# A shared expert in high and low products, and a router spread over other chunks of the step

## The chip, the cores and the metric

The kernel runs on one core of a Trainium2 chip. The metric is the device time of one execution in microseconds (us). The engines named are TensorE (PE, its weight loads PEld), VectorE (DVE), ScalarE (ACT), GpSimd (POOL) and SyncE (SP), whose queue issues most DMA transfers.

## What is computed

The input x is 128 sequences of 128 rows of 256 numbers, and so is the context. The layer is a cross attention with a difference of two softmaxes, and then a mixture of experts with two chosen of 16 and one shared expert. Cut to what matters:

```python
x = x + xattn(ctx, layernorm(x))          # 32 half heads of 8, 16 heads
x = x + moe(layernorm(x))

def moe(x):
    shared = silu(x @ ws_gate) * (x @ ws_up) @ ws_down
    scores = sigmoid(x @ gate_w.T)
    topk_w, topk_idx = top_k(scores, 2)
    topk_w = topk_w / (topk_w.sum(-1) + 1e-20) * 2.5
    routed = sum over the two chosen experts of topk_w * expert(x)
    return routed + shared
```

The change concerns `shared`, `scores` and the choice of the two experts.

## The kernel before

The work has two parts. The first and longer one is a software pipeline over 64 pairs of sequences (256 rows each). A step of it runs the attention of one pair `it` and, beside it, earlier and later stages of other pairs: the projections of pair it + 3 (called a), the values and the maxima of pair it + 1 (b), the second normalization of pair it - 1 (d), and the router and shared expert of pair it - 2 (r). The second part runs the routed experts over 288 tiles of rows; the change does not touch it.

Each step has 16 chunks, k = 0 to 15. In every chunk TensorE first does four products for the maxima of pair b (L493, bank `mx_ps`) and four for the scores of pair it (L486, bank `st_ps`), which stand alternately. VectorE reduces the first to maxima (L981), ScalarE takes the exponential of the second (L825). In odd chunks TensorE then multiplies with the values (L526, eight records in the trace). After that comes the side work of the chunk, written in `side(it, k)` for TensorE, and in a `step` function of its own for each other engine. Each engine runs its list strictly in order; counting semaphores tie the lists together. The banks for scores and maxima are double, so TensorE in chunk k needs the maxima of chunk k - 2 reduced.

Two more banks of PSUM, `ms_ps` 0 and 1 (M0 and M1 in the code), are shared by all side work in turn. `clear(it, bank, n)` makes TensorE wait for whoever read the bank last. M0 holds in turn the values of pair b, the logits, the result of the shared down layer, the ranks, and the keys of pair a. M1 holds the transposed rows of pair a, the shared gate and up results, the queries of pair a, and the transposed normalized rows of pair d.

The side work that matters here, before the change:

- chunk 2: a transpose of maxima (L542), which ScalarE copies (L797) and SyncE sends by DMA (L369) into the stacks of the scores; TensorE waits for it to land ahead of chunk 8.
- chunk 3: the gate layer of the shared expert (L575, two full float32 products over the two halves of the input rows; they show as four records), then the logits (L582).
- chunk 4, 7, 12, 15: four transposes of attention outputs (L537).
- chunk 5: the up layer (L575). ScalarE takes tanh of the gate (L854), VectorE makes the hidden layer in its chunk 6 with two instructions (L1025 to `sh_g`, L1028 to `sh_h`), which read M1, and the best two experts in chunk 7 (L1040 to L1048), the choice in chunk 8 (L1053), the addition of the down result to the residual in chunk 9 (L1035).
- chunks 8 and 9: the down layer, one full product each (L605), into M0.
- chunks 9 and 10: the query projection of pair a into M1, each a set of six products of high and low parts (L554, L555, L556, twice). Such a set is already used for all three attention projections and for the routed experts.
- chunk 11: the ranks (L601, L602). Chunks 13 and 14: the key projection into M0.

`product` multiplies high by high, high by low and low by high parts of rounded operands. The high parts are copies by ScalarE into the rounded type, the low parts differences by VectorE or GpSimd. The bank rule of M1 reads:

```python
"M1": (((v_x, 1, a, 1),), ((v_sh, 1, r, 1),), ((v_q, 1, a, 1),), ((a_h, 1, d, 1),)),
```

Its second entry is the wait ahead of the query projection: for the hidden layer of pair r.

Of the kernel before, what the change touches and what calls it, by code (L numbers as in the profile page):

```python
# [13 lines left out]
ALU = mybir.AluOpType  # L14
# [51 lines left out]
def program(nc, x, ctxT, lq1, lk1, lq2, lk2, wqT, wkT, wvT, gate_wT, w_gu, w_dn, ws_gu, ws_dn, out):  # L66
# [31 lines left out]
    with ExitStack() as st:  # L98
# [19 lines left out]
        ws_dn_sb = sb("ws_dn_sb", [P, D])  # L118
        in_lo = e_lo[:, :, :, :].rearrange("p e k n -> p (e k n)")
# [127 lines left out]
        v_rt, v_hot, v_pf, v_pos, v_next = sem("v_rt"), sem("v_hot"), sem("v_pf"), sem("v_pos"), sem("v_next")  # L247
# [5 lines left out]
        v_base, g_ve1, g_ve2 = sem("v_base"), sem("g_ve1"), sem("g_ve2")  # L253
# [3 lines left out]
        N_SPLIT = 3  # L257
# [74 lines left out]
        split_w = [(w_in[:, n, :, :], w_hi[:, n, :, :], w_lo[:, n, :, :]) for n in range(3)]  # L332

# [141 lines left out]
        def _(pe):  # L475
            pe.wait_ge(d_w, 16 * N_W)
            pe.wait_ge(g_set, SETUP)
            pe.wait_ge(v_wl, N_SPLIT)
# [107 lines left out]
            def clear(it, bank, n):  # L586

                a, b, d, r = it.plus(3), it.plus(1), it.plus(-1), it.plus(-2)
                users = {"M0": (((a_v, 1, b, 1),), ((a_e, 1, r, 1),), ((v_base, 1, r, 1),), ((v_pf, 1, r, 1),),
                                ((a_k, 2, a, 2),)),  # L590
                         "M1": (((v_x, 1, a, 1),), ((v_sh, 1, r, 1),), ((v_q, 1, a, 1),), ((a_h, 1, d, 1),)),
# [12 lines left out]
            def shared_down(bank, u):  # L604
                return pe.matmul(bank[:, u * D:(u + 1) * D], sh_h[:, u * P:(u + 1) * P], ws_dn_sb[:, :], start=True, stop=True)  # L605

            def finish():
# [6 lines left out]
                pe.wait_ge(v_sh, NS - 1)  # L614
# [15 lines left out]
                pe.wait_ge(v_sh, NS)  # L630
# [5 lines left out]
            def side(it, k):  # L636
# [15 lines left out]
                alone = it.k is None and it.off >= NS  # L652
                if k == 3 and do_r:
                    wait(pe, a_h, 1, r, 1)
                    if alone:
                        clear(it, "M0", 1)
                        route()
                if k in (3, 5) and do_r:
                    if k == 3:
                        clear(it, "M1", 1)  # L660
                    mm = gate_up(k // 2 - 1)
                    if k == 5:
                        mm.then_inc(p_su, 1)
# [804 lines left out]
```

## Time and profile before

| | us |
|---|---|
| median of 3 runs | 2138.11 |
| lowest and highest | 2124.88, 2149.83 |
| profiled execution | 2130.88 |
| its span, first to last instruction | 2129.1 |
| TensorE busy | 1967.5 (92%) |
| VectorE, ScalarE, GpSimd busy | 1616.4, 1464.5, 1441.6 |

The trace gives each instruction's start and length on its engine, and for idle time ahead of an instruction what ended it. Matmuls overlap in the engine, so what one costs is read from the start of one to the start of the next, and not from its length.

### The profile page before, as it was taken

The numbers are of one execution on the slowest core, as the hardware profiler recorded it, in microseconds if no ns is written. First come the engines' busy times: TensorE is split into PE (matmuls) and PEld (weight loads), VectorE is DVE, ScalarE is ACT, GpSimd is POOL, SyncE is SP. The second block draws the span as 40 slices with busy tenths as digits, with TensorE's granted clock in tenths as the row PEclk, the third lists the DMA queues.
The fourth block names the chain that finished last, engine by engine and source line by source line (L and its number), as shares of the span: only waits on it lengthen the run. The fifth ranks groups of instructions, "written<-read, shape, count | busy, mean of one in ns | idle before, by whom it ended". The sixth has DMA issues, their size and how long they took to land.

```text
span 2129.1 us, 76257 instructions
## 1 busy us (share of the span) xinstructions
PE 1967.5 (92%) x20840; PEld 1418.7 (67%) x20840; DVE 1616.4 (76%) x4623; ACT 1464.5 (69%) x3511; POOL 1441.6 (68%) x2183
## 2 busy tenths in 40 slices
PE   3899999999999999999999999999989699999997
PEld 2555666666666666666666666666655599989996
DVE  2667788888778878888788887778776777767775
ACT  2567778777778777787787877777766455545554
POOL 4346677777677777677777777777656566656665
PEclk8799999999999999999999999999999799999999
DMA  4766676667666767666667676666774688868885
GB/s 122 195 189 194 186 199 189 203 203 199 190 185 196 204 189 196 194 195 194 198 194 201 190 200 193 192 190 191 212 211 161 206 266 263 259 200 274 256 267 172
DMA packets 606681, 432.00 MB, mean 203 GB/s; under 512 B 437572, under 2 KB 552395, under 8 KB 606161
## 3 DMA queue, kind: packets, MB, share of 16 engines
q1 hardware_dynamic: 546288, 319.87, 54.4%
q0 software_dynamic: 32256, 84.47, 10.9%
q10 hardware_dynamic: 28000, 26.03, 4.0%
q8 instruction: 64, 1.05, 0.2%
q14 instruction: 73, 0.59, 0.1%
HBM read 234.59 MB, written 197.72 MB: 203 GB/s over the span
## 4 chain that ended last, share of the span: by engine, by line
PE 54%; DMA 15%; SPq 14%; issue 7%; DVE 6%; POOL 3%; ACT 1%; DVEq 0%; POOLq 0%; ACTq 0%
DMA stacks<-mxT 8%; PE mx_ps L493 8%; SPq L369 7%; PE o_ps L526 6%; PE ms_ps L777 5%; PE ms_ps L554 5%; SPq L361 3%; SPq L354 3%; DMA stack_dram<-w_dn_sb 3%; PE mx_ps L554 3%; DMA stacks<-stack_dram 3%; PE mx_ps L556 3%; PE mx_ps L555 3%; PE ms_ps L555 3%; PE st_ps L755 3%
## 5 line engine op out<-in xcount | busy, mean ns | idle before, releaser
L981 DVE TENSOR_REDUCE mx<-mx_ps 128x4 f32<-128x512 f32 x1024 | 696.6, 686 | 234.4 <-PE mx_ps L493 229.7
L825 ACT ACTIVATE prob<-st_ps 128x512 f32<-128x512 f32 x1024 | 607.7, 596 | 318.4 <-PE st_ps L486 299.0
L493 PE MATMUL mx_ps<-stacks 48*128 48x128 bf16 x4096 | 397.7, 221 | 84.3 <-DMA stacks<-mxT 62.9
L486 PE MATMUL st_ps<-stacks 50*128 50x128 bf16 x4096 | 397.0, 221 | 0.0
L493 PEld LDWEIGHTS mx_ps<-stacks 48*128 48x128 bf16 x4096 | 232.4, 95 | 240.6 <-issue 130.5
L526 PE MATMUL o_ps<-prob,v_sb 128*32 128x256 f32 x4096 | 334.0, 398 | 0.9 <-ACT oT L812 0.6
L1343 POOL DMA_INDIRECT rows_dram<-rowt,posi x256 | 253.7, 991 | 67.9 <-issue 63.7
L554 PE MATMUL ms_ps<-e_lo 128*128 128x256 f32 x768 | 269.5, 351 | 18.6 <-DVE rowt L1080 9.8
L486 PEld LDWEIGHTS st_ps<-stacks 50*128 50x128 bf16 x4096 | 230.6, 95 | 2.6 <-issue 1.5
L555 PE MATMUL ms_ps<-e_lo 128*128 128x256 f32 x768 | 222.8, 290 | 0.0
L556 PE MATMUL ms_ps<-e_lo 128*128 128x256 f32 x768 | 221.8, 289 | 0.0
L554 PEld LDWEIGHTS ms_ps<-e_lo 128*128 128x128 f32 x768 | 151.0, 197 | 100.3 <-issue 44.6
L922 ACT ACTIVATE rows_T<-st_ps 128x256 fp32r<-128x256 f32 x288 | 110.7, 385 | 140.0 <-PE st_ps L755 136.8
L1412 POOL DMA_INDIRECT sums_dram<-stacks x144 | 141.7, 984 | 81.2 <-issue 65.4
L1416 POOL DMA_INDIRECT out<-stacks x144 | 141.7, 984 | 79.3 <-issue 64.3
L554 PE MATMUL mx_ps<-e_hi,rows_T 128*128 x576 | 188.2, 327 | 0.0
L1206 DVE TENSOR_TENSOR rows_lo<-st_ps,rows_T 128x256 fp32r<-128x256 f32 x288 | 122.3, 425 | 80.9 <-ACT rows_T L922 59.1
L1349 POOL DMA_INDIRECT base_dram<-base_t,posi x128 | 139.1, 1087 | 53.0 <-issue 51.0
L777 PE MATMUL ms_ps<-w_dn_sb,v_sb 128*128 x576 | 172.8, 382 | 0.4 <-DVE stacks L1219 0.3
L537 PE MATMUL o_ps<-ident,oT 128*128 128x128 f32 x1024 | 168.1, 287 | 0.6 <-issue 0.4
L556 PE MATMUL mx_ps<-e_hi,rows_lo 128*128 x576 | 163.7, 284 | 0.0
L555 PE MATMUL mx_ps<-e_lo,rows_T 128*128 x576 | 163.4, 284 | 0.0
(155 smaller groups left out, 4667.3 us busy)
## 6 DMA issues: line engine op xcount, KB each, us to landing
stacks<-stack_dram SPq DMA_DIRECT2D x512, 192.0 KB
stack_dram<-w_dn_sb SPq DMA_DIRECT2D x192, 256.0 KB
stacks<-rows_dram SPq DMA_DIRECT2D x288, 130.0 KB
stack_dram<-w_dn_sb SPq DMA_DIRECT2D x64, 384.0 KB
stack_dram<-w_dn_sb SPq DMA_DIRECT2D x192, 128.0 KB
w_dn_sb<-in_x SPq DMA_DIRECT2D x64, 256.0 KB
w_dn_sb<-in_ctxT SPq DMA_DIRECT2D x64, 256.0 KB, 3.2
x_res<-in_x SPq DMA_DIRECT2D x64, 256.0 KB
```

Source lines behind the costliest of these rows:

```text
L369: sp.dma_start(q_st[s.par()][row:row + 2, u, :, :], mxT[u][2 * SHH * h:2 * SHH * (h + 1), :]).then_inc(d_m[u], 16)
L486: return pe.matmul(st_ps[k % 2][:, i * P:(i + 1) * P], k_st[p][64 * h:64 * h + KROWS, u, j, :], q_st[p][64 * h:64 * h + KROWS, u, j, :], s ...
L493: return pe.matmul(mx_ps[k % 2][:, i * P:(i + 1) * P], q_st[p][64 * h:64 * h + ROWS, u, j, :], k_st[p][64 * h:64 * h + ROWS, u, j, :], sta ...
L526: mm = pe.matmul(OT[SLOT * g:SLOT * (g + 1), gg * SW:(gg + 1) * SW], v_sb[s.par()][:, (u * HEADS + 2 * c + i) * SLOT:(u * HEADS + 2 * c + ...
L537: mm = pe.transpose(out_ps, src, ident[:, :])
L554: pe.matmul(out_ps, rnd(still[0]), rnd(moving[0]), start=start, stop=False)
L555: pe.matmul(out_ps, rnd(still[0]), rnd(moving[1]), start=False, stop=False)
L556: return pe.matmul(out_ps, rnd(still[1]), rnd(moving[0]), start=False, stop=stop)
L777: pe.matmul(eo_ps[t.off % 2][:, 0:D], hid_T[t.off % 4][:, :], w_dn_sb[:, bass.ds(down, 1), :].rearrange("p e n -> p (e n)"), start=True, s ...
L825: nc.scalar.activation(prob[k % 4][:, :], st_ps[k % 2][:, :], ACT.Exp, scale=float(HALF) ** -0.5).then_inc(a_exp, 1)
L981: v.tensor_reduce(mx[:, u, c * CHUNK:(c + 1) * CHUNK], mx_ps[k % 2][:, :].rearrange("p (c n) -> p c n", c=CHUNK), AX.X, ALU.max).then_inc( ...
L1343: g.indirect_dma_start(rows_dram[k][:, :], bass.IndirectOffsetOnAxis(ap=posi[p][:, u, k:k + 1], axis=0), rowt[p][:, u, :], None).then_inc( ...
```

## The change

The three layers of the shared expert become sets of products of high and low parts. New tiles are `gu_hi`, `gu_lo`, `dn_hi`, `dn_lo` for the weights (split once, early), `h2_hi`, `h2_lo` for the normalized rows, and `sh_hi`, `sh_lo` for the hidden layer. ScalarE makes the high part of the rows in its chunk 2, ahead of the copy of maxima, and that of the hidden layer in its chunk 9. GpSimd makes the low part of the rows (`normed_low`) after its third residual piece, VectorE the low part of the hidden layer in its chunk 10.

On TensorE the logits go from chunk 3 to chunk 4, gate and up from 3 and 5 to 5 and 6, the ranks from 11 to 9, and the down layer, both halves together, from 8 and 9 to 12. On VectorE the best two go to chunk 6, the choice to 7, the hidden layer to 8, the places from 12 to 10, the positions from 13 to 11, the addition from 9 to 12. Semaphores that were no longer needed are merged.

```diff
@@ gate_up, TensorE
-                    mm = pe.matmul(M1[:, k * SW:(k + 1) * SW], ws_gu_sb[:, h, k * HID:(k + 1) * HID], h2T[:, h, :],
-                                   start=(h == 0), stop=(h == DK - 1))
+                    mm = product(M1[:, k * SW:(k + 1) * SW], [w[:, h, k * HID:(k + 1) * HID] for w in (gu_hi, gu_lo)],
+                                 [x[:, h, :] for x in (h2_hi, h2_lo)], h == 0, h == DK - 1)
@@ clear
-                         "M1": (((v_x, 1, a, 1),), ((v_sh, 1, r, 1),), ((v_q, 1, a, 1),), ((a_h, 1, d, 1),)),
+                         "M1": (((v_x, 1, a, 1),), ((v_sh, 2, r, 1),), ((v_q, 1, a, 1),), ((a_h, 1, d, 1),)),
@@ side, TensorE
+                if k in (5, 6) and do_r:
+                    if k == 5:
+                        clear(it, "M1", 1)
...
+                        wait(pe, a_hh, 1, r, 1)
+                        wait(pe, g_hl, 1, r, 1)
+                    mm = gate_up(k - 5)
...
-                if k in (8, 9) and do_r:
-                    if k == 8:
-                        clear(it, "M0", 2)
-                        wait(pe, v_sh, 1, r, 1)
-                    mm = shared_down(M0, k - 8)
...
+                if k == 12 and do_r:
+                    clear(it, "M0", 3)
+                    wait(pe, a_sh, 2, r, 2)
+                    wait(pe, v_sh, 2, r, 2)
+                    for u in range(2):
+                        mm = shared_down(M0, u)
+                    mm.then_inc(p_sd, 1)
@@ ScalarE
+                    if k == 2 and do_r:
+                        wait(act, a_h, 1, r, 1)
+                        wait(act, p_su, 1, r)
+                        nc.scalar.activation(rnd(h2_hi[:, :, :]), h2T[:, :, :], ACT.Copy).then_inc(a_hh, 1)
...
+                    if k == 9 and do_r:
+                        wait(act, v_sh, 2, r, 1)
+                        wait(act, p_sd, 1, r)
+                        nc.scalar.activation(rnd(sh_hi[:, :]), sh_h[:, :], ACT.Copy).then_inc(a_sh, 1)
@@ VectorE
+            def shared_low(s):
+                wait(dve, a_sh, 2, s, 2)
                 wait(dve, p_sd, 1, s)
-                v.scalar_tensor_tensor(sh_h[:, :], sh_g[:, :], 0.5, M1[:, SW:2 * SW], ALU.mult, ALU.mult).then_inc(v_sh, 1)
+                v.tensor_tensor(rnd(sh_lo[:, :]), sh_h[:, :], sh_hi[:, :], ALU.subtract).then_inc(v_sh, 1)
@@ step, VectorE
                     if k in COMBINE_AT and do_c:
                         combine(it, COMBINE_AT.index(k))
                     if k == 8 and do_r:
-                        choice(r)
-                    if k == 9 and do_r:
-                        shared_add(r, M0)
+                        shared_hidden(r)
@@ GpSimd
+            def normed_low(s):
+
+                wait(gp, a_hh, 1, s, 1)
+                wait(gp, p_su, 1, s)
+                g.tensor_tensor(rnd(h2_lo[:, :, :]), h2T[:, :, :], h2_hi[:, :, :], ALU.subtract).then_inc(g_hl, 1)
```

The order in which the instructions stand shows three places. The first is TensorE in the steady loop, chunk 3 and the side work of chunk 4 before; `ms_ps` is a side bank, `h2T` the normalized rows, `gw_sb` the router's weights.

```order
L281 REGISTER_ALU [waits a_v]
L526 MATMUL o_ps<-prob,v_sb 32x256 [waits a_o]
...
L281 REGISTER_ALU [waits a_h]
L575 MATMUL ms_ps<-h2T,ws_gu_sb 128x256 [waits v_x]
...
L582 MATMUL ms_ps<-gw_sb,h2T 128x16 [waits a_v]
...
L281 REGISTER_ALU [waits d_stk00,a_exp]
L493 MATMUL mx_ps<-stacks 128x128 [waits v_red]
```

And the same place in the changed kernel, whose lines are others:

```order
L286 REGISTER_ALU [waits a_v]
L532 MATMUL o_ps<-prob,v_sb 32x256 [waits a_o]
...
L286 REGISTER_ALU [waits d_stk00,a_exp]
L499 MATMUL mx_ps<-stacks 128x128 [waits v_red]
...
L286 REGISTER_ALU [waits a_h]
L588 MATMUL ms_ps<-gw_sb,h2T 128x16 [waits a_v]
...
L543 MATMUL o_ps<-ident,oT 128x128 [waits a_o,a_mT]
```

The logits stood behind the gate layer and ahead of chunk 4's maxima; now nothing stands between the product with the values and chunk 4, and the logits, with their wait for `a_v`, come behind its maxima and scores.

The second place is TensorE in chunks 8 and 9, before, from the last transpose of chunk 7; `e_lo` stands for the operands of the query projection, which lie in that tile.

```order
L281 REGISTER_ALU [waits d_stk11,a_exp]
L493 MATMUL mx_ps<-stacks 128x128 [waits d_m1,v_red]
...
L605 MATMUL ms_ps<-ws_dn_sb,sh_h 128x256 [waits v_sh,a_e]
...
L605 MATMUL ms_ps<-ws_dn_sb,sh_h 128x256
L554 MATMUL ms_ps<-e_lo 128x256 [waits v_x,v_sh]
L555 MATMUL ms_ps<-e_lo 128x256
```

And now:

```order
L286 REGISTER_ALU [waits d_stk11,a_exp]
L499 MATMUL mx_ps<-stacks 128x128 [waits d_m1,v_red]
...
L532 MATMUL o_ps<-prob,v_sb 32x256 x4
L286 REGISTER_ALU
L560 MATMUL ms_ps<-e_lo 128x256 [waits v_x,v_sh]
L561 MATMUL ms_ps<-e_lo 128x256
...
L607 MATMUL ms_ps<-hot,upper 128x64 [waits v_hot,a_e]
L608 MATMUL ms_ps<-hot,onesb 128x64
```

The two down products are gone from here, the ranks stand behind the projection, and the projection's wait for `v_sh` is the first wait in the row for that semaphore.

The third place is VectorE in its chunks 6 to 9, before:

```order
L1025 SCALAR_TENSOR_TENSOR sh_g<-sh_t,ms_ps 128x256 [waits a_sh]
L1028 SCALAR_TENSOR_TENSOR sh_h<-sh_g,ms_ps 128x256 [waits p_sd,v_sg]
...
L981 TENSOR_REDUCE mx<-mx_ps 128x4 [waits p_mx]
L1040 TENSOR_REDUCE ez<-ez 128x32 [waits a_e]
...
L981 TENSOR_REDUCE mx<-mx_ps 128x4 [waits v_mx,p_mx]
...
L999 RECIPROCAL rl<-o_ps 128x16 [waits v_cb,p_o]
L1002 TENSOR_TENSOR o_sc<-o_ps,rl 128x256 [waits g_att,v_rl]
...
L1053 TENSOR_TENSOR hot<-iota_e,topi 128x64 [waits v_rt]
```

And now:

```order
L1067 TENSOR_REDUCE ez<-ez 128x32 [waits a_e]
...
L1002 TENSOR_REDUCE mx<-mx_ps 128x4 [waits p_mx]
...
L1080 TENSOR_TENSOR hot<-iota_e,topi 128x64 [waits v_rt]
...
L1002 TENSOR_REDUCE mx<-mx_ps 128x4 [waits v_mx,p_mx]
...
L1020 RECIPROCAL rl<-o_ps 128x16 [waits v_cb,p_o]
L1023 TENSOR_TENSOR o_sc<-o_ps,rl 128x256 [waits g_att,v_rl]
L1046 SCALAR_TENSOR_TENSOR sh_g<-sh_t,ms_ps 128x256 [waits a_sh]
L1050 SCALAR_TENSOR_TENSOR sh_h<-sh_g,ms_ps 128x256 [waits v_sh,a_sh,v_sg]
```

The two instructions of the hidden layer moved from the head of this row to its end, behind the best two, the choice, the maxima of chunk 8 and a combine (the reciprocal and the product after it).

## Rows read from the trace of the kernel before

**Rows 1.** The page: busy us, share of the span and instructions of each engine.

```profile
PE 1967.5 (92%) x20840; PEld 1418.7 (67%) x20840; DVE 1616.4 (76%) x4623; ACT 1464.5 (69%) x3511; POOL 1441.6 (68%) x2183
```

**Rows 2.** Groups by line and shape, 600 to 1400 us: count, busy us, mean ns.

```profile
L981 DVE TENSOR_REDUCE mx<-mx_ps 128x4 f32<-128x512 f32 x524 | 357.3, 687 | 90.3 <-PE mx_ps L493 87.7 <-issue 1.1
...
L1301 POOL TENSOR_TENSOR e_lo<-w_dn_sb,e_lo 128x512 fp32r<-128x512 f32 x33 | 41.8, 1268 | 2.8 <-ACT e_lo L860 2.8
...
L860 ACT ACTIVATE e_lo<-w_dn_sb 128x512 fp32r<-128x512 f32 x33 | 20.8, 629 | 0.0
```

**Rows 3.** Waits, 600 to 1400 us: us in total, times, longest.

```profile
POOL ve L1282 <- DVE mv L1020: 69.1, 32, 3.8
...
PE mx_ps L493 <- DMA stacks<-mxT: 27.8, 33, 2.3
```

**Rows 4.** Timeline of TensorE, one step: start, length, instruction, idle before it.

```profile
1229.87 0.23 PE L493 MATMUL mx_ps<-stacks 48*128 48x128 bf16 x1
...
1231.73 0.96 PE L582 MATMUL ms_ps<-gw_sb,h2T 128*128 128x16 f32 x8
1232.63 0.23 PE L493 MATMUL mx_ps<-stacks 48*128 48x128 bf16 x1
...
1232.96 0.66 PE L537 MATMUL o_ps<-ident,oT 128*128 128x128 f32 x4
1233.54 0.23 PE L493 MATMUL mx_ps<-stacks 48*128 48x128 bf16 x1
...
1234.44 1.13 PE L575 MATMUL ms_ps<-h2T,ws_gu_sb 128*128 128x256 f32 x4
1235.50 0.23 PE L493 MATMUL mx_ps<-stacks 48*128 48x128 bf16 x1
...
1238.00 0.21 PE L493 MATMUL mx_ps<-stacks 48*128 48x128 bf16 x1 [0.72 <-DMA stacks<-mxT]
...
1238.33 0.70 PE L605 MATMUL ms_ps<-ws_dn_sb,sh_h 128*128 128x256 f32 x2
1238.96 0.23 PE L493 MATMUL mx_ps<-stacks 48*128 48x128 bf16 x1
...
1240.20 0.47 PE L554 MATMUL ms_ps<-e_lo 128*128 128x256 f32 x1
...
1241.52 0.38 PE L554 MATMUL ms_ps<-e_lo 128*128 128x256 f32 x1
...
1242.43 0.24 PE L542 MATMUL o_ps<-identb,mxp 128*64 128x128 bf16 x1
...
1244.59 0.23 PE L493 MATMUL mx_ps<-stacks 48*128 48x128 bf16 x1
```

**Rows 5.** Timeline of VectorE, the same step.

```profile
1235.93 0.69 DVE L981 TENSOR_REDUCE mx<-mx_ps 128x4 f32<-128x512 f32 x1 [0.28 <-PE mx_ps L493]
1236.54 0.41 DVE L1025 SCALAR_TENSOR_TENSOR sh_g<-sh_t,ms_ps 128x256 f32<-128x256 f32 x1
1236.99 0.42 DVE L1028 SCALAR_TENSOR_TENSOR sh_h<-sh_g,ms_ps 128x256 f32<-128x256 f32 x1
...
1237.93 0.21 DVE L1040 TENSOR_REDUCE ez<-ez 128x32 f32<-128x64 f32 x1
...
1239.39 0.67 DVE L981 TENSOR_REDUCE mx<-mx_ps 128x4 f32<-128x512 f32 x1
1239.98 0.25 DVE L999 RECIPROCAL rl<-o_ps 128x16 f32<-128x16 f32 x1
...
1240.61 0.21 DVE L1053 TENSOR_TENSOR hot<-iota_e,topi 128x64 bf16<-128x64 f32 x1
1240.74 0.68 DVE L981 TENSOR_REDUCE mx<-mx_ps 128x4 f32<-128x512 f32 x1
```

**Rows 6.** Timeline of ScalarE, the same step: the copy of the values.

```profile
1230.83 0.59 ACT L838 ACTIVATE v_sb<-ms_ps 128x512 f32<-128x512 f32 x1
```

**Rows 7.** Timeline of GpSimd, the same step: the last instruction of the residual.

```profile
1232.36 0.45 POOL L1328 TENSOR_TENSOR x<-att,x_res 128x128 f32<-128x128 f32 x1 [0.18 <-POOL att L1321]
```

More of the change, by code:

```diff
@@ L118, in program @@
         ws_dn_sb = sb("ws_dn_sb", [P, D])
+        gu_hi, gu_lo = (sb(f"gu_{n}", [P, DK, 2 * HID]) for n in ("hi", "lo"))
+        dn_hi, dn_lo = (sb(f"dn_{n}", [P, D]) for n in ("hi", "lo"))
         in_lo = e_lo[:, :, :, :].rearrange("p e k n -> p (e k n)")
@@ L165, in program @@
         h2T = sb("h2T", [P, DK, SW])
+        h2_hi, h2_lo = (sb(f"h2_{n}", [P, DK, SW]) for n in ("hi", "lo"))
         sh_t = sb("sh_t", [P, SW])
@@ L168, in program @@
         sh_h = sb("sh_h", [P, SW])
+        sh_hi, sh_lo = (sb(f"sh_{n}", [P, SW]) for n in ("hi", "lo"))
         lam_in = sb("lam_in", [P, 4, HALF])
@@ L604, in shared_down @@
             def shared_down(bank, u):
-                return pe.matmul(bank[:, u * D:(u + 1) * D], sh_h[:, u * P:(u + 1) * P], ws_dn_sb[:, :], start=True, stop=True)
+                return product(bank[:, u * D:(u + 1) * D], [x[:, u * P:(u + 1) * P] for x in (sh_hi, sh_lo)],
+                               [w[:, :] for w in (dn_hi, dn_lo)], True, True)
             def finish():
@@ L832, in step @@
                         copy_out(d, 3)
+                    if k == 8 and it.k is None and it.off == -1:
+                        for weights, high, _ in split_ws:
+                            nc.scalar.activation(rnd(high), weights, ACT.Copy).then_inc(a_wh, 1)
+                    if k == 2 and do_r:
+                        wait(act, a_h, 1, r, 1)
+                        wait(act, p_su, 1, r)
+                        nc.scalar.activation(rnd(h2_hi[:, :, :]), h2T[:, :, :], ACT.Copy).then_inc(a_hh, 1)
                     if k == 2 and do_c:
@@ L841, in step @@
                                              ACT.Copy).then_inc(a_v, 1)
-                    if k == 4 and do_r:
+                    if k == 5 and do_r:
                         wait(act, p_lg, 1, r, 1)
@@ L850, in step @@
                         copy_out(it, 0)
-                    if k == 5 and do_r:
+                    if k == 7 and do_r:
                         wait(act, p_su, 1, r, 1)
@@ L1124, in step @@
                         stats(xs, x_in, bs1, mv1, v_b1, v_s1, a_n1)
+                    if k == 3 and it.k is None and it.off == 0:
+                        for n, (weights, high, low_part) in enumerate(split_ws):
+                            dve.wait_ge(a_wh, len(split_w) + n + 1)
+                            v.tensor_tensor(rnd(low_part), weights, high, ALU.subtract).then_inc(v_wl, 1)
                     if k == 4 and do_d:
@@ L1196, in _ @@
             v.tensor_scalar(expert_tab[:, :], o_ps[0][0:1, 0:N_ALL], float(E - 1), None, ALU.min).then_inc(v_row, 1)
+            shared_low(last)
             shared_add(last, mx_ps[1])
```

82 lines of the change are left out of this document (43 added, 39 removed).

## The prediction

> **What bounds the kernel now.** I read first the busy shares [rows 1]: TensorE is busy for 92% of the span, every other engine for 76% or less. So the question is where TensorE waits and what a change of its order does to those waits. The stretch from 600 to 1400 us is the steady loop. Its groups of instructions [rows 2] hold 524 reductions of maxima, 16 to a step, so 32.75 steps in 800 us: 24.43 us a step. The waits of the same stretch [rows 3] name two that come once a step. TensorE waits 27.8 us in 33 times, 0.84 us a step and at most 2.3, at chunk 8 for the transfer that brings the transposed maxima. GpSimd waits 69.1 us in 32 times, 2.16 us a step, for the row statistics; that is its reserve. The rest of the 24.43 us is TensorE's own work with small waits for VectorE.
>
> Then I read one step on TensorE [rows 4]. Chunk 3 begins at 1229.87, chunk 4 at 1232.63, chunk 5 at 1233.54, chunk 6 at 1235.50, chunk 8 at 1238.00 after a wait of 0.72, chunk 9 at 1238.96, chunk 13 at 1244.59. Start to start these rows also give the prices: scores and maxima of a chunk 0.33 (1232.63 to 1232.96); these and the product with the values 0.90 (1233.54 to 1234.44); four transposes 0.58; the logits 0.90 (1231.73 to 1232.63); one gate or up layer, as two full products, 1.06; the first down product 0.63 (1238.33 to 1238.96), the second 0.34 (1238.96 + 0.90 = 1239.86, next work 1240.20); one set of six high and low products 0.91 (1241.52 to 1242.43). VectorE in the same step [rows 5]: it gets a chunk's maxima 0.43 us after TensorE starts the chunk (1235.50, 1235.93), needs 0.61 for them, 0.87 from the start of the shared hidden layer's first instruction to the end of its second (1236.54 to 1236.99 + 0.42), 1.46 for the best two (1237.93 to 1239.39), 0.59 for the next maxima, 0.63 for a combine (1239.98 to 1240.61), and 0.13 for the choice.
>
> **The change part by part.**
>
> 1. The products themselves. Each of three layers (gate, up, down) becomes a set of six. Gate and up go from 1.06 to 0.91 each, at most 0.15 gained twice; the down layer from 0.63 + 0.34 = 0.97 to 0.91. TensorE's own work falls by about 0.36 us a step. The row shows a saving of 6 to 14% in a set. [...]
>
> 2. Chunks 3 to 7. The logits move from chunk 3 to chunk 4, the gate layer to chunk 5, the up layer to chunk 6. New times, from 1229.87: chunk 3 has 0.90, so chunk 4 begins at 1230.77, and its logits are ready to go at 1231.10. They write the bank that ScalarE still copies the values from, 1230.83 + 0.59 = 1231.42 [rows 6]. Before, the gate layer hid this; now it is a wait of about 0.37. Then 1231.47 + 0.90 + 0.58: chunk 5 at 1232.95, its gate layer at 1233.85. This needs the low part of the normalized rows, which GpSimd makes in a new instruction; the nearest row takes 1.27 [rows 2]. GpSimd is free of the residual at 1232.36 + 0.45 = 1232.81 [rows 7], so the low part is there at about 1234.1: a wait of 0 (if GpSimd runs earlier in the longer step) to 0.3. Chunk 6 at 1234.76, chunk 7 at 1236.00, chunk 8 ready at 1236.00 + 0.90 + 0.58 = 1237.48, with the wait 1237.8. Before, TensorE was ready at 1238.00 - 0.72 = 1237.28. So nothing is gained ahead of chunk 8, and as the transfer came at 1238.00, nothing is lost there either.
>
> ScalarE's new high part (0.60 to 0.63, [rows 2] has 0.63 for the same size) stands ahead of the copy of the maxima for that transfer; ScalarE was idle there, so I cost it at nothing, and at up to 0.15 if that cover is too short. GpSimd's 1.27 a step fits into its 2.16.
>
> 3. Chunks 8 to 13: here the sum is made. The gate and up results lie in the bank that the next query projection, in chunk 9, will overwrite. TensorE therefore waits in chunk 9 for VectorE's second instruction of the shared hidden layer. Before, VectorE did this in its chunk 6, done at 1237.4 at the latest [rows 5], three microseconds before the projection at 1240.20: no wait. Now it stands in VectorE's chunk 8, behind the maxima of chunk 8 and a combine. Working: chunk 6 begins at 1234.76, its maxima reach VectorE at 1235.19; + 0.61 + 1.46 (best two) + 0.59 (maxima 7) + 0.13 (choice) = 1237.98. The maxima of chunk 8 are there at 1238.00 + 0.43 = 1238.43, so VectorE is in time; + 0.59 + 0.63 (combine) + 0.87 (the two instructions to the end of the second) = 1240.52, seen by TensorE at 1240.57. TensorE itself, without the down products, stands before the projection at 1238.00 + 0.33 + 0.90 = 1239.23. It waits 1.34 us. Behind it in TensorE's queue are the scores of every later chunk, for which ScalarE and VectorE wait, so nothing of it is hidden.
>
> From chunk 8 to chunk 13 the step took 1244.59 - 1238.00 = 6.59. Now: 6.59 - 0.97 (old down) + 0.91 (new down, in chunk 12) + 1.34 = 7.87, less about 0.09 of weight load that no longer follows a down product: 7.78, or 1.19 more. The rank products stay inside this stretch.
>
> 4. What comes back. Chunk 8 waits for the transfer 0.84 us in the mean. SyncE starts the large loads that run ahead of it when the last scores of the old step are done; in a longer step SyncE arrives earlier relative to that, so the transfer may land earlier. Fully gone, the wait gives back what lies between 1238.00 and 1237.48 plus the surplus of the mean, 0.5 to 0.6; not gone, nothing. VectorE's queue allows at most 0.44 of it, since it is not through its chunk 7 before 1237.98. I take 0.3, half of that range.
>
> 5. Later in the step, the key projection in chunk 13 waits for the addition that reads the down result; TensorE is there at 1238.00 + 7.78 + 0.90 = 1246.68. The down result is out at about 1245.8, and an addition of the nearest size (a 128x512 reduction, 0.69 in [rows 2]) ends at about 1246.6. So 0 to 0.3, the end for a VectorE that is behind. VectorE's low part (0.41) and ScalarE's high part of the hidden layer fall where TensorE waits anyway.
>
> Sum: 1.19 - 0.3 = 0.9 us a step, bounds 0.5 (all given back, work a little cheaper) and 1.5 (nothing given back, 0.3 at chunk 5 or 13). The projection and the shared layers are both there in 59 steps of the 64 (the first two and last three have only one of them). 59 x 0.9 = 53 us. The longer chain for the last pair adds about 1 us: 54. The profiled execution took 2130.9 us (span 2129.1), so 2185; the median of the runs is 7 us above it, 2192. I give 2190.
>
> **Rivals.**
>
> A. The products decide: no wait in chunk 9 that counts, and the 0.36 us of TensorE's work come through. 64 x 0.36 = 23 us less, about 2113. For it: TensorE is at 92%. Against: the wait in chunk 9 follows from the written orders and measured rows; it would need VectorE 1.3 us earlier. [...] Chance 0.06.
>
> B. The transfer's wait pays for all of it: 0.84 a step goes, and the new wait is under 0.8, so that steps come out at -0.1 to +0.3: 2130 to 2155. For it: the wait is there in every step. Against: VectorE is the one late in chunk 9, whether or not the transfer is. Chance 0.14.
>
> C. GpSimd becomes the bound: its new instruction and its serial chain from the statistics to the low part make the gate layer wait by over 1 us a step as well, on top of the wait in chunk 9: 1.19 + 0.8 = 2 us, 118 us, about 2250. For it: the instruction comes right ahead of its consumer. Against: 2.16 us of reserve. Chance 0.11.
>
> **How the numbers follow.** The forecast has 0.69 with its own range 2165 to 2225 (0.5 to 1.5 a step above the median, rounded). The range to hold 8 in 10 adds the upper part of B and some of C: 2145 to 2232. A measurement tells about 1% (21 us) from no change. Faster by over 1%: A's larger half, 0.04. Within 1%: the rest of A and most of B, 0.14. Slower: 0.82, which is the forecast, C and the upper end of B.
>
> **What would show it.** In the trace after: a wait of TensorE in front of the first query product of 1.0 to 1.4 us in nearly every step, put down to VectorE's second hidden instruction; the chunk 8 wait for the transfer below 0.84; the six gate products at 0.91; logits waiting 0.3 to 0.4 for ScalarE's copy of the values; a step of 25.0 to 25.6 us. If that first wait is under 0.5, the forecast falls; if GpSimd's wait for the statistics is gone, C holds.

## The result and the profile after

The changed kernel takes 2337.1 us (median of 3 runs, 2327.6 to 2339.6) against 2138.1: a ratio of 1.092, 95% interval 1.081 to 1.104. It is slower, as forecast, but by about 199 us where I had 52. The time lies outside my range.

**The step.** The first view is the groups of the changed kernel by line and shape, 600 to 1400 us, which answers to [rows 2]. The columns are the count, busy us and mean ns of one, and the idle time before with its releasers.

```profile
L1002 DVE TENSOR_REDUCE mx<-mx_ps 128x4 f32<-128x512 f32 x460 | 315.9, 687 | 136.1 <-PE mx_ps L499 127.4 <-issue 7.9
...
L1080 DVE TENSOR_TENSOR hot<-iota_e,topi 128x64 bf16<-128x64 f32 x29 | 36.7, 1264 | 0.0
```

There are 460 reductions of maxima, 16 to a step: 28.75 steps in 800 us, 27.83 us a step where it was 24.43. Measured on TensorE from the first product of the side work of chunk 0 to that of the next step, 27 steps have a mean of 27.77 (the kernel before: 32 steps, 24.44). The difference of 3.34 us times 59 is 197 us, so the loop accounts for the whole result. The last row already shows something I had not priced: the choice of the experts takes 1.26 us in the mean. I had allowed it 0.13 of VectorE's time, from the distance of two starts in [rows 5], where its duration is 0.21. The steady loop of both kernels was read on one profiled execution each.

**The waits.** The same stretch, answering to [rows 3]; us in total, times, longest.

```profile
POOL x L1367 <- DVE base_t L1062: 73.2, 28, 3.6
PE ms_ps L560 <- DVE sh_h L1050: 66.6, 29, 2.4
...
POOL ve L1315 <- DVE mv L1041: 42.5, 29, 2.6
...
PE ms_ps L588 <- ACT v_sb L854: 8.9, 29, 0.3
...
PE ms_ps L560 <- POOL h_lo L1340: 8.5, 29, 1.9
```

TensorE waits 66.6 / 29 = 2.30 us a step for VectorE's second hidden instruction: the wait that I forecast, at the place I forecast, but not 1.34. The two small waits are there as forecast: 0.31 in the mean for ScalarE's copy of the values, 0.29 for GpSimd's low part (most are about 0.24, one is 1.9). TensorE's wait of [rows 3] for the transfer of the maxima is gone. GpSimd keeps 1.47 us of its reserve ahead of the statistics, and spends 2.6 more behind the base addition, which now comes late; TensorE waits for it only the 0.29, so it is not the bound.

**Why 2.30 and not 1.34.** VectorE of the changed kernel in one step, from the maxima of chunk 6 to the hidden layer. The columns are start, length, instruction, and in brackets the idle time before it.

```profile
1022.39 0.69 DVE L1002 TENSOR_REDUCE mx<-mx_ps 128x4 f32<-128x512 f32 x1 [0.83 <-PE mx_ps L499]
1023.00 0.21 DVE L1067 TENSOR_REDUCE ez<-ez 128x32 f32<-128x64 f32 x1
...
1024.46 0.67 DVE L1002 TENSOR_REDUCE mx<-mx_ps 128x4 f32<-128x512 f32 x1
1025.05 1.29 DVE L1080 TENSOR_TENSOR hot<-iota_e,topi 128x64 bf16<-128x64 f32 x1
1026.26 0.68 DVE L1002 TENSOR_REDUCE mx<-mx_ps 128x4 f32<-128x512 f32 x1
...
1028.08 0.42 DVE L1050 SCALAR_TENSOR_TENSOR sh_h<-sh_g,ms_ps 128x256 f32<-128x256 f32 x1 [0.19 <-DVE sh_g L1046]
```

GpSimd in the same microseconds:

```profile
1022.81 1.16 POOL L1351 TENSOR_TENSOR w_dn_sb<-k_rest,w_dn_sb 128x512 bf16<-128x512 f32 x1
...
1024.57 0.45 POOL L1367 TENSOR_TENSOR x<-att,x_res 128x128 f32<-128x128 f32 x1 [0.18 <-POOL att L1360]
1024.98 1.27 POOL L1334 TENSOR_TENSOR e_lo<-w_dn_sb,e_lo 128x512 fp32r<-128x512 f32 x1
```

And TensorE:

```profile
1025.51 0.64 PE L532 MATMUL o_ps<-prob,v_sb 128*32 128x256 f32 x8
1028.55 0.39 PE L560 MATMUL ms_ps<-e_lo 128*128 128x256 f32 x1 [2.40 <-DVE sh_h L1050]
```

The order of VectorE is the one I had written down, and every length but one is as in [rows 5]. The choice starts 0.07 us after GpSimd's context low part and ends 0.09 after it: 1025.05 + 1.29 = 1026.34 against 1024.98 + 1.27 = 1026.25. It ended when that instruction had ended, as if it had stood still beside it. The maxima at 1024.46 run beside the same instruction and the one ahead of it, read PSUM, and keep their length of 0.67. The reduction at 1023.00, which has one SBUF input, runs beside GpSimd's instruction of 1.16 us at 1022.81 and keeps its 0.21. In the kernel before, the choice at 1240.61 fell on GpSimd's indirect DMA (1239.66 to 1240.75) and took 0.21. The excess is 1.29 - 0.21 = 1.08, and 1.34 + 1.08 = 2.42, the 2.40 of this step.

The two need not start together. In the second run of this kernel (below) one step has the choice 0.54 us behind the start of GpSimd's instruction. It then takes 0.81 and ends 0.08 after it, and TensorE's wait in that step is 1.39:

```profile
1173.81 1.27 POOL L1334 TENSOR_TENSOR e_lo<-w_dn_sb,e_lo 128x512 fp32r<-128x512 f32 x1
1174.35 0.81 DVE L1080 TENSOR_TENSOR hot<-iota_e,topi 128x64 bf16<-128x64 f32 x1
```

So in these two rows the choice lasts as long as what is left of GpSimd's instruction (1.20 and 0.73 us), and 0.09 and 0.08 more.

The choice has two inputs in SBUF (the expert numbers and the chosen indices) and took 1.29 beside GpSimd's instruction, 0.21 without. That the number of inputs matters was my assumption, also in the expectations below, and is not shown: no run here varies it alone. And not every GpSimd instruction makes one with two SBUF inputs longer: VectorE's low part of the hidden layer, `sh_lo`, kept its 0.41 us at 780.19, beside GpSimd's `mv` of 128x2 (0.72 us).

**Why 3.34 a step.** With the wait at 2.30, my own sum becomes 0.9 + 0.96 = 1.9 a step, not 3.34. With all of the transfer's 0.84 given back, and not 0.3, it is 1.3. The rest is the clock. Stretches one microsecond wide of the same step; behind the busy times of the engines stands the granted clock (PEclk), then the DMA share and GB/s.

```profile
1029.00:1030.00 1.00, 1.00 (x11) 0.82 (x11) 0.61 (x3) 0.58 (x2) 0.03 (x1) 0.55 1.06 331
1030.00:1031.00 1.00, 1.00 (x11) 0.80 (x8) 0.53 (x1) 0.50 (x1) 0.82 (x2) 0.50 0.22 84
1031.00:1032.00 1.00, 1.00 (x6) 0.78 (x5) 1.00 (x8) 0.10 (x1) 0.66 (x3) 0.50 0.35 45
1032.00:1033.00 1.00, 1.00 (x18) 0.57 (x17) 0.60 (x5) 0.20 (x1) 0.97 (x1) 0.74 0.26 106
```

TensorE stands still from 1026.15 to 1028.55, goes on, and from 1029.1 its granted clock is at half (0.50) until 1032.5. It loses 0.45 + 0.50 + 0.50 + 0.26 = 1.7 us of full-speed time there, though it is busy all through (1.00 in each microsecond above). This step is 27.4 us long. In the next one the clock falls for twice as long, at half from 1057 to 1063 and for parts of the microseconds around, and the step is 28.4 us long:

```profile
1057.00:1058.00 1.00, 1.00 (x11) 0.80 (x8) 0.56 (x1) 0.52 (x1) 0.72 (x2) 0.50 0.38 148
...
1062.00:1063.00 1.00, 1.00 (x6) 1.00 (x5) 0.65 (x2) 0.97 (x2) 0.00 (x0) 0.50 0.13 35
```

One step of the stretch is spared. It begins at 1182.10, waits 2.41 like the others, its clock stays at 1.00, and it is 25.88 long, 1.9 below the mean of the 27 and 1.45 above the 24.43 of before, near the 1.3 of the sum above. Its wait and the clock behind it:

```profile
1197.62 0.39 PE L560 MATMUL ms_ps<-e_lo 128*128 128x256 f32 x1 [2.41 <-DVE sh_h L1050]
```

```profile
1197.00:1203.00 6.00, 5.38 (x69) 4.08 (x73) 5.51 (x20) 4.18 (x10) 3.77 (x8) 1.00 0.56 159
```

Of the other 26 steps, the 14 whose clock is at half for 3.4 us have a mean of 27.26, the 12 with 6.8 us one of 28.52.

Over 600 us of the loop, first the changed kernel, then the kernel before, the granted clock again third from the right, 0.92 against 0.99:

```profile
760.00:1360.00 600.00, 534.05 (x6119) 362.96 (x6113) 465.59 (x1275) 431.30 (x932) 419.06 (x652) 0.92 0.62 172
```

```profile
760.00:1360.00 600.00, 573.39 (x6794) 381.32 (x6792) 487.69 (x1419) 464.31 (x1009) 440.67 (x713) 0.99 0.68 195
```

### The profile page after: what moved, and what is told of

It is laid out like the page before. It is cut to its first block, busy times and chain, and to the rows that moved or that the text cites. A ratio compares the mean times of both kernels' runs of the same rounds, so it can differ in the third digit from the quotient of the medians.

```text
span 2325.9 us, 77880 instructions
## 1 busy us (share of the span) xinstructions
PE 2052.2 (88%) x21224; PEld 1502.4 (65%) x21224; DVE 1711.8 (74%) x4689; ACT 1528.0 (66%) x3641; POOL 1529.0 (66%) x2247
## 3 DMA queue, kind: packets, MB, share of 16 engines
q8 instruction: 65, 1.06, 0.2%
## 4 chain that ended last, share of the span: by engine, by line
PE 42%; issue 20%; POOL 16%; DVE 9%; ACT 6%; DMA 3%; SPq 1%; POOLq 1%; DVEq 0%; ACTq 0%
PE ms_ps L560 6%; POOL rows_dram L1382 6%; PE mx_ps L499 6%; PE ms_ps L786 5%; PE ms_ps L562 3%; PE ms_ps L561 3%; POOL h_lo L1340 3%; PE o_ps L532 3%; PE mx_ps L560 3%; PE mx_ps L562 3%; PE mx_ps L561 3%; POOL k_rest L1346 3%; PE st_ps L764 3%; POOL att L1360 2%; DVE mx L1002 2%
## 5 line engine op out<-in xcount | busy, mean ns | idle before, releaser
L499 PE MATMUL mx_ps<-stacks 48*128 48x128 bf16 x4096 | 431.9, 231 | 34.0 <-DMA stacks<-mxT 15.8
L492 PE MATMUL st_ps<-stacks 50*128 50x128 bf16 x4096 | 431.7, 231 | 0.0
L560 PE MATMUL ms_ps<-e_lo 128*128 128x256 f32 x768 | 282.2, 367 | 142.2 <-DVE sh_h L1050 124.7
L499 PEld LDWEIGHTS mx_ps<-stacks 48*128 48x128 bf16 x4096 | 245.8, 99 | 225.7 <-issue 111.8
L532 PE MATMUL o_ps<-prob,v_sb 128*32 128x256 f32 x4096 | 348.6, 414 | 0.6 <-ACT prob L834 0.4
L560 PEld LDWEIGHTS ms_ps<-e_lo 128*128 128x128 f32 x768 | 163.0, 212 | 254.9 <-DVE sh_h L1050 150.7
L492 PEld LDWEIGHTS st_ps<-stacks 50*128 50x128 bf16 x4096 | 245.7, 99 | 3.5 <-ACT prob L834 1.8
L1367 POOL TENSOR_TENSOR x<-att,x_res 128x128 f32<-128x128 f32 x256 | 117.2, 458 | 195.6 <-DVE base_t L1062 163.1
L562 PE MATMUL ms_ps<-e_lo 128*128 128x256 f32 x768 | 242.3, 316 | 0.0
L561 PE MATMUL ms_ps<-e_lo 128*128 128x256 f32 x768 | 240.7, 313 | 0.0
L543 PE MATMUL o_ps<-ident,oT 128*128 128x128 f32 x1024 | 177.8, 299 | 1.1 <-issue 1.1
L562 PEld LDWEIGHTS ms_ps<-e_lo 128*128 128x128 f32 x768 | 170.8, 222 | 0.0
```

The costliest lines, as they stand in the source:

```text
L492: return pe.matmul(st_ps[k % 2][:, i * P:(i + 1) * P], k_st[p][64 * h:64 * h + KROWS, u, j, :], q_st[p][64 * h:64 * h + KROWS, u, j, :], s ...
L499: return pe.matmul(mx_ps[k % 2][:, i * P:(i + 1) * P], q_st[p][64 * h:64 * h + ROWS, u, j, :], k_st[p][64 * h:64 * h + ROWS, u, j, :], sta ...
L532: mm = pe.matmul(OT[SLOT * g:SLOT * (g + 1), gg * SW:(gg + 1) * SW], v_sb[s.par()][:, (u * HEADS + 2 * c + i) * SLOT:(u * HEADS + 2 * c + ...
L543: mm = pe.transpose(out_ps, src, ident[:, :])
L560: pe.matmul(out_ps, rnd(still[0]), rnd(moving[0]), start=start, stop=False)
L561: pe.matmul(out_ps, rnd(still[0]), rnd(moving[1]), start=False, stop=False)
```

## The experiments

So there were three theories of the loss, which can all hold at once. P: the place of the hidden layer makes the wait. C: the choice, blocked by GpSimd, makes it larger. K: the wait makes the clock fall. All kernels start from the changed kernel.

**First set, another chip.** Four edits were run together. First, the hidden layer ahead of the choice in VectorE's chunk 7:

```
                     if k == 7 and do_r:
+                        shared_hidden(r)
                         choice(r)
...
-                    if k == 8 and do_r:
-                        shared_hidden(r)
```

> The changed kernel with one edit: VectorE makes the shared hidden layer in its chunk 7, ahead of the choice, and not in chunk 8 behind a combine. Theory P (the place of the hidden layer in VectorE's queue holds TensorE in chunk 9, and all else of the loss follows from that idle time): the 2.4 us ahead of the query product go to under 0.4, the granted clock of the steady loop goes from about 0.91 back to 0.98 or more, and a step falls from 27.8 to 24.0 to 24.6 us; time 2105 to 2150. Rival G (GpSimd, which now waits for the late addition of the down result and makes the low part just ahead of its use, is the bound): the wait in chunk 9 goes but the gate layer waits longer for the low part; a step stays above 26, time above 2230.

Second, the choice behind the hidden layer, both in chunk 8:

```
-                    if k == 7 and do_r:
-                        choice(r)
...
                     if k == 8 and do_r:
                         shared_hidden(r)
+                        choice(r)
```

> The changed kernel with one edit: the choice stands behind the hidden layer in VectorE's chunk 8, and not in chunk 7. In the changed kernel it takes 1.29 us where it took 0.22 before, and ends 0.1 us after GpSimd's low part of the context ends. Theory C (a VectorE instruction with two SBUF operands cannot run while GpSimd's low part of the context does): the choice, now about 2.5 us later, is at 0.2 to 0.3 us, and the wait in chunk 9 falls from 2.4 to about 1.2. Without theory C (the place of the choice alone counts) the wait falls by 0.13, to 2.3, and the choice still takes 1.2 or more wherever it stands. On the clock: if it falls because of an idle stretch of over 2 us ahead of it, a wait of 1.2 leaves it at 0.97 or more, a step is at 25.0 to 25.6 and the time at 2165 to 2210; if the clock falls in spite of the shorter wait, a step is at 26 to 27.

Third, GpSimd's two instructions exchanged, so that the low part of the context comes after the choice:

```
+                if do_b:
+                    first_maxima(b)
                 if do_a:
                     context_low(a)
-                if do_b:
-                    first_maxima(b)
```

> The changed kernel with one edit on GpSimd alone: the first maxima are copied ahead of the low part of the context, so that the latter begins about 0.9 us later; VectorE's order is untouched. Theory C: the choice no longer falls into the low part of the context and takes 0.2 to 0.4; the wait in chunk 9 goes from 2.4 to 1.2 to 1.5, with a time like that of the kernel with the choice moved, 2165 to 2230. Without C: the choice still takes 1.2 or more, time within 1% of 2337.

Fourth, 18 useless products for TensorE in the place of the wait, into the bank that the ranks overwrite next; nothing that is read is changed:

```
                     if k == 9:
+                        if do_r:
+                            clear(it, "M0", 2)
+                            for _ in range(18):
+                                pe.matmul(M0[:, 0:D], rnd(dn_hi[:, 0:P]), rnd(dn_hi[:, :]), start=True, stop=True)
                         clear(it, "M1", 2)
```

> The changed kernel with 18 products of no use on TensorE in chunk 9, ahead of the query product, into a bank that is free there (no result depends on them). At 0.12 us each they fill about 2.1 of the 2.4 us of idle time and delay nothing. Theory K (the idle stretch makes the granted clock fall to half for 3 to 7 us, and that is about half of the loss): the clock of the steady loop is at 0.98 or more, a step goes from 27.8 to 25.8 to 26.1 us though TensorE has more to do, and the time from 2337 to 2215 to 2240. Rival (the longer products behind the wait are slow for another reason, as operands that other engines use at the time): they stay slow, and the time stays within 1% of 2337 or rises.

Measured: 2376.7 us (ratio 1.041, interval 1.037 to 1.044), 2452.3 (1.076, 1.072 to 1.080), 2478.9 (1.085, 1.083 to 1.088) and 2514.8 (1.100, 1.095 to 1.104). But on this chip the kernel before took 2282.3 us, 144 more than on the first, and none of the four times lies in the range of the theory that it was to test, which was worked out for the first chip. Other waits are there: in the first kernel TensorE waits up to 1.2 us a time for ScalarE's copy of the values, where it was 0.3 in the changed kernel on the first chip.

```profile
PE ms_ps L588 <- ACT v_sb L854: 31.3, 27, 1.2
```

Within the set the kernel with the early hidden layer is the fastest, which favours P. The choice no longer falls on GpSimd's instruction even in the kernel with the useless products, where the order leaves them together: 219 ns. GpSimd's instruction comes later there, since it waits up to 1.8 us a time for ScalarE's high part.

```profile
L1084 DVE TENSOR_TENSOR hot<-iota_e,topi 128x64 bf16<-128x64 f32 x27 | 5.9, 219 | 0.0
```

Nothing here can be set against 1.092, since the changed kernel itself was not in the set. The set is inconclusive on C and K, and the second edit was not tried again. Why this chip is slower stays open; I have no trace of the kernel before from it.

One reading of it bears on K. In the first kernel's steps TensorE waits 0.51 us ahead of chunk 4 and 1.16 ahead of the logits, 1.6 us later, and behind that the clock is at half from 809.09 to 812.50:

```profile
807.98 1.06 PE L588 MATMUL ms_ps<-gw_sb,h2T 128*128 128x16 f32 x8 [1.16 <-ACT v_sb L854]
```

```profile
809.00:813.00 4.00, 4.00 (x35) 2.49 (x34) 1.46 (x4) 1.44 (x4) 3.15 (x6) 0.57 0.66 150
```

From 600 to 1400 us 27 of 29 steps have such a fall. So a wait much shorter than 2.3 us can also be followed by a fall.

**Second set, with a control.** The changed kernel unaltered and three of the four edits again. The chip gave 2139.0 us for the kernel before, like the first.

> The changed kernel itself, unaltered, as the yardstick beside the three runs that follow; the first four experiments ran on a chip on which the kernel before took 2282 us instead of 2138, so they cannot be set against 2337. All theories: a ratio of 1.08 to 1.10 to the kernel before if the chip is like the first, and the same 2.3 us ahead of the query product; if the ratio is under 1.06, the loss depends on the chip.

> The changed kernel with the hidden layer in VectorE's chunk 7, ahead of the choice. Theory P (its place in VectorE's queue is the cause of the whole loss): ratio to the kernel before 0.985 to 1.01, clock of the steady loop 0.98 or more, no wait over 0.4 us ahead of the query product. Rival G (GpSimd's longer chain is the bound): ratio above 1.03 with that wait gone.

> The changed kernel with GpSimd's first maxima ahead of its low part of the context, VectorE's order untouched. Theory C (the choice, with two SBUF operands, waits while GpSimd's low part of the context runs): choice 0.2 to 0.4 us instead of 1.29, wait ahead of the query product 1.2 to 1.5 instead of 2.3, and with a shorter idle stretch the clock at 0.95 or more; ratio 1.02 to 1.05. Without C: ratio that of the unaltered kernel within 1%.

> The changed kernel with 18 useless products on TensorE in the idle time ahead of the query product. Theory K (the idle stretch halves the clock behind it, which is about half of the loss): clock of the steady loop 0.98 or more and ratio 1.03 to 1.06, so 4 to 6% under the unaltered kernel though TensorE does more. Rival: the products behind the wait stay slow; ratio that of the unaltered kernel or above.

| kernel | us | ratio, 95% interval | step, us | clock, profiled run |
|---|---|---|---|---|
| changed, unaltered | 2330.7 | 1.090, 1.084 to 1.095 | 28.03 | 0.905 |
| hidden layer in chunk 7 | 2149.2 | 1.005, 1.003 to 1.008 | 24.41 | 0.967 |
| GpSimd exchanged | 2194.9 | 1.028, 1.023 to 1.034 | 25.25 | 0.957 |
| useless products | 2215.9 | 1.036, 1.032 to 1.040 | 26.00 | 0.971 |

The step is the mean of 27 to 32 steps, from 600 to 1400 us. The control repeats the result. P holds: with the hidden layer early, the loss goes from 9.0% to 0.5%, and rival G, GpSimd as the bound with a ratio above 1.03, falls. TensorE's waits in that kernel, 600 to 1400 us:

```profile
PE ms_ps L560 <- DVE base_t L1062: 21.3, 33, 0.7
...
PE mx_ps L499 <- DMA stacks<-mxT: 6.9, 12, 0.9
```

The wait for the hidden layer is gone from the list, and the transfer's wait of [rows 3] is back in part.

C holds: with GpSimd's instructions exchanged the choice is short again and the wait falls to 40.6 / 32 = 1.27.

```profile
PE ms_ps L560 <- DVE sh_h L1050: 40.6, 32, 1.5
```

```profile
L1080 DVE TENSOR_TENSOR hot<-iota_e,topi 128x64 bf16<-128x64 f32 x32 | 6.9, 216 | 0.0
```

This is the kernel that I had priced without knowing it: a wait of 1.27 for my 1.34, a step of 25.25 for my 25.3, 2194.9 us for my 2190. The wait was worked out, but that the step and the time fit so well is in part luck: 27 of the 31 steps kept their clock and have a mean of 24.80, and four with the clock at half for 6.8 to 10.2 us (27.6 to 29.4 us long) make the rest. At this wait the clock mostly holds, 0.99 in the same stretch of the loop:

```profile
760.00:1360.00 600.00, 551.98 (x6757) 374.82 (x6756) 485.69 (x1414) 472.48 (x1031) 459.20 (x720) 0.99 0.66 189
```

K holds: with TensorE kept busy, the choice is as slow as in the changed kernel and the hidden layer as late, and still each step is 28.03 - 26.00 = 2.0 us shorter. The choice, the second hidden instruction and the first query product, and then the clock of the loop, in the kernel with the useless products:

```profile
1014.93 1.30 DVE L1084 TENSOR_TENSOR hot<-iota_e,topi 128x64 bf16<-128x64 f32 x1
...
1017.98 0.42 DVE L1054 SCALAR_TENSOR_TENSOR sh_h<-sh_g,ms_ps 128x256 f32<-128x256 f32 x1 [0.19 <-DVE sh_g L1050]
...
1018.45 0.39 PE L560 MATMUL ms_ps<-e_lo 128*128 128x256 f32 x1
```

```profile
760.00:1360.00 600.00, 583.18 (x6951) 410.74 (x6949) 493.85 (x1372) 456.96 (x996) 442.44 (x696) 1.00 0.64 184
```

More work, less time. The useless products end at 1018.37, the hidden layer at 1018.40, and the query product starts at 1018.45, as soon after it as in the changed kernel; this is so in nearly every step, so they delay almost nothing.

The 3.6 us that a step of the control is above the 24.43 of before come apart best over the steps whose clock stayed up all through. Their means are 24.19 in the kernel before (29 of 32 steps), 24.80 with GpSimd exchanged (27 of 31) and 25.79 with useless products (28 of 30). The place of the hidden layer with a short choice so costs 0.6, the blocked choice 1.0 more, which is the difference of the two waits, 2.30 - 1.27. The fallen clock costs the other 28.03 - 25.79 = 2.2, against 0.24 that it already cost in the kernel before (24.43 - 24.19). The kernel before was not profiled in this set; its steps are those of the first chip.

**Third set: is there more to gain, and what is the product form worth?** The kernel with the early hidden layer is the base here, run again.

> The changed kernel with the shared expert's hidden layer ahead of the choice in VectorE's chunk 7, as before; it is the base of the three other kernels of this call. 2149 us as in the earlier call, 1.0054 of the kernel before; in its steps TensorE waits 0.31 us ahead of the logits for ScalarE's copy of the values and some 0.6 us ahead of the key projection for VectorE's base add.

Then the base addition ahead of the query's rest, to take away the wait that had come up in the chunk of the key projection:

```
+                    if k == 12 and do_r:
+                        shared_add(r, M0)
                     if k == 12 and do_a:
                         rest(a, M1, a_q, qp, q_rest, g_qs, v_q)
-                    if k == 12 and do_r:
-                        shared_add(r, M0)
```

> The same, with the base add ahead of the query's rest in VectorE's chunk 12. Theory A (the wait ahead of the key projection is on the path): the add ends 0.6 us earlier, the key projection starts 0.6 us earlier in each of 59 steps, 35 us less: some 2114 us, 0.989 of the kernel before. Theory B (the DMA of the maxima's stacks, or VectorE, which in these steps is busy from chunk 5 on, pays it back at the next place): under 10 us less, 2140 to 2150, with the wait of TensorE found in chunk 8 for the stacks or at the scores for VectorE's reduction.

Then, on top of it, the logits behind the turn of the fourth output:

```
-                if k == 4 and do_r:
-                    wait(pe, a_h, 1, r, 1)
-                    clear(it, "M0", 1)
-                    route()
...
                 if k == 4 and do_d:
                     clear(it, "TO", 1)
                     turn_out(d, 3)
+                if k == 4 and do_r:
+                    wait(pe, a_h, 1, r, 1)
+                    clear(it, "M0", 1)
+                    route()
```

> The same as the last, and the logits behind the turn of the fourth output in chunk 4, so that ScalarE's copy of the values is through by then. Theory A: 0.31 us less in each of 59 steps, 18 us below the last kernel: some 2096 us, 0.98 of the kernel before. Theory B: the same time as the last kernel within 6 us.

And the base with the three layers as full products again:

```
-                    mm = product(M1[:, k * SW:(k + 1) * SW], ...
+                    mm = pe.matmul(M1[:, k * SW:(k + 1) * SW], ws_gu_sb[:, h, k * HID:(k + 1) * HID], h2T[:, h, :],
+                                   start=(h == 0), stop=(h == DK - 1))
...
-                return product(bank[:, u * D:(u + 1) * D], ...
+                return pe.matmul(bank[:, u * D:(u + 1) * D], sh_h[:, u * P:(u + 1) * P], ws_dn_sb[:, :], start=True, stop=True)
```

> The first of this call (hidden layer in chunk 7), with the shared expert's three layers again as full float32 products of the unsplit operands, the split still made on the other engines but not read. It measures the product form alone. The prediction's first part (a full set costs 0.06 to 0.15 us more than six products, 0.36 us a step, all of it on TensorE's path): 21 us more than the first, some 2170 us, 1.015 of the kernel before. Rival (that time is hidden behind the waits for the base add and the stacks): within 6 us of the first.

Measured, against 2138.0 for the kernel before: the base 2151.5 us (1.007, 1.004 to 1.010), the early addition 2144.3 (1.003, 1.001 to 1.005), with the logits moved too 2151.8 (1.005, 1.002 to 1.007), full products 2151.1 (1.006, 1.003 to 1.008). For the early addition and the full products the second expectation of the pair came true. With the logits moved neither did: 18 us less or the same within 6 us was expected, and the median is 7.6 us higher, though the two intervals overlap. No version beats the kernel before.

TensorE's waits in the base, 600 to 1400 us:

```profile
PE ms_ps L560 <- DVE base_t L1062: 18.7, 31, 0.7
PE mx_ps L499 <- DMA stacks<-mxT: 14.7, 18, 2.0
```

with the early addition:

```profile
PE mx_ps L499 <- DMA stacks<-mxT: 27.8, 33, 1.9
PE ms_ps L588 <- ACT v_sb L854: 10.2, 33, 0.4
PE ms_ps L560 <- POOL h_lo L1339: 6.1, 11, 2.4
```

and with the logits moved as well:

```profile
PE mx_ps L499 <- DMA stacks<-mxT: 29.3, 34, 1.8
PE ms_ps L560 <- POOL h_lo L1339: 12.0, 17, 2.3
PE mx_ps L499 <- DVE mx L1002: 7.8, 17, 0.9
```

The wait for the addition goes (18.7 us less), and 13.1 of it come back as the wait for the transfer of the maxima, the 27.8 of [rows 3]; 2.7 more are ahead of GpSimd's low part. For the next 10 us, ahead of the logits, 5.9 come back as waits for GpSimd's low part and 6.7 as waits for VectorE's maxima. With full products a layer does take longer. In the first rows (full products) from the gate layer to the up layer it is 705.57 - 704.17 = 1.40 us, in the second (base) 697.20 - 695.97 = 1.23; both contain the scores of one chunk:

```profile
704.17 1.13 PE L581 MATMUL ms_ps<-h2T,ws_gu_sb 128*128 128x256 f32 x4
705.57 1.13 PE L581 MATMUL ms_ps<-h2T,ws_gu_sb 128*128 128x256 f32 x4
```

```profile
695.97 0.38 PE L560 MATMUL ms_ps<-h_hi,gu_hi 128*128 128x256 f32 x1
...
697.20 0.38 PE L560 MATMUL ms_ps<-h_hi,gu_hi 128*128 128x256 f32 x1
```

These 0.17 us twice a step do not appear in the time, 2151.1 against 2151.5. In the full product kernel TensorE waits less instead:

```profile
PE ms_ps L560 <- DVE base_t L1061: 15.1, 32, 0.6
...
PE mx_ps L499 <- DMA stacks<-mxT: 7.8, 12, 0.9
```

That is 3.6 less for the addition and 6.9 less for the transfer. A part is left all the same: over the steps whose clock stayed up, the median is 24.46 us with full products and 24.30 in the base, 0.16 of the 0.34. Such steps are 29 of 31 there and 27 of 31 in the base, and that difference, which may be chance, covers it in the mean (24.72 and 24.67). So at about 24.4 us a step most of what is taken from TensorE's work or waits comes back as another wait, mostly for the transfer of the maxima. What sets its arrival (the SyncE queue, the DMA load, or the chain of maxima that leads to it) was not tried.

## Why the prediction was wrong in size

Direction and mechanism of the wait were right: the wait in chunk 9 for the second hidden instruction is there in every step, with it gone the loss is gone, and no rival held. It was about 0.96 us too short, and what followed from its length was not in the sum. By its own steps:

- Part 1, the products: the price was right (0.17 a layer measured, 0.15 forecast), the conclusion was too simple. I counted 0.36 us as gained on the path, within the chunk times of parts 2 and 3; the full product experiment shows it worth 0.16 in a quiet step without the wait, and nothing in the time. With the wait, part of it only moves TensorE's arrival. Here a product of rounded parts takes 0.12 us from start to start inside a set, against 1.06 / 2 = 0.53 for a full one. A set of six costs 0.91 and not 6 x 0.12 because its first and last take 0.2 each (the changed kernel, 1010.20 to 1011.11); why is not shown.
- Part 2: right in both waits. Logits wait 0.31 for 0.37; gate layer 0.29 for 0 to 0.3.
- Part 3, the sum's main term: **the step that failed is "+ 0.13 (choice)"**. I took it from a row in which GpSimd was at an indirect DMA, and did not ask what GpSimd does where the choice was moved to. [rows 2] has its 1.27 us instruction, and the order of the new kernel puts it there. With 1.29 minus 0.21 the wait is 2.42 instead of 1.34; 2.30 in the mean was measured. The exchanged kernel shows that all else in this part was right (1.27).
- Part 4, what comes back: the transfer's wait went altogether, 0.84 instead of the 0.3 that I took. That made the step about 0.5 shorter than my sum had it, and hid a part of the error in part 3.
- Part 5: nothing, as at the low end forecast; TensorE is so late that the addition is through. It came up, with 0.6 a step, only where the big wait was gone.
- **A term is missing:** the granted clock. I treated an idle TensorE as a loss of just that idle time. Behind a wait of 2.1 to 2.4 us the granted clock fell to half (0.50) for 3.4 to 6.8 us in 55 of 56 such waits (both runs of the changed kernel, 600 to 1400 us), and that costs 2.0 us a step or a little more, more than the place (0.6) or the blocked choice (1.0). Behind the waits of 1.2 to 1.5 us in the exchanged kernel it fell in 3 of 32, so with part 3 right little of the missing term would have shown. The trace of the kernel before had the sign: in 3 of 32 steps TensorE waited 1.45 to 2.29 us for the transfer, the clock behind it was at half for 3.4 us, and the step took 26.3 to 27.1. One of them is shown below this list. The range, built from bounds of each term alone, had no room for an error that brings another cost with it.
- The rivals: A needed the wait to be absent, B below 0.8. C needed GpSimd's statistics reserve to go; 1.47 of 2.16 is left. GpSimd mattered by what ran beside the choice, and not through its queue. Counted from 2138, A's 2113 should be 2115 and C's 2250 should be 2256; nothing hangs on it.

The kernel before, one of its three steps with a fallen clock: TensorE's wait and the clock behind it.

```profile
1311.74 0.21 PE L493 MATMUL mx_ps<-stacks 48*128 48x128 bf16 x1 [2.29 <-DMA stacks<-mxT]
```

```profile
1313.00:1317.00 4.00, 4.00 (x29) 2.76 (x26) 2.50 (x8) 1.43 (x4) 0.19 (x1) 0.57 0.94 227
```

## What to carry to other kernels

When a VectorE instruction is moved, look up what GpSimd does at the new place; here the choice (128x64, two inputs in SBUF, 0.21 us) took 1.29 and 0.81 beside GpSimd's low part (128x512, 1.27 us) and ended 0.09 and 0.08 after it. Price a new TensorE wait with the clock that may follow it, and look in the trace of before for waits that were followed by a fall; the length of one wait does not tell it alone (2.41 us without a fall on one chip, 1.16 with one on another). And before shaving a TensorE wait or product in a loop, see whether another wait of the same step takes the time back: here three such edits changed the time by 0.4% at most.

## What the runs showed of the hardware that was not expected

- A VectorE instruction of 0.21 us took 1.29 beside a GpSimd instruction of 1.27; exchanging two GpSimd instructions gave back 6.2 points of the 9.0 (1.090 to 1.028): 2.8 us a step, of which 1.0 is the wait itself and the rest the clock.
- Two waits that look alike (2.41 and 2.40 us, in the steps from 1182.10 and 1012.92) were followed by a clock of 1.00 and by 3.4 us at half. The step lengths fall into groups at 25.9, 27.0 to 27.4 and 28.4 to 28.5, as the clock fell not at all, for 3.4 or for 6.8 us; one of 28.95 has a wait of 1.91 for GpSimd's low part besides. What decides between them stays open.
- Eighteen useless products a step made the kernel 115 us faster (2330.7 to 2215.9).
- The same kernel before took 2282.3 us on one chip and 2139.0 on another. A ratio from one is not to be set against a ratio from the other: the same kernel with the early hidden layer is at 1.041 on the one and at 1.005 on the other.
